# One state in sixteen of a selective scan joins its neighbour's tile on VectorE before TensorE sums them

## The reference

```python
dA = jnp.exp(dt[..., None] * A)                       # 512 positions x 512 features x 16 states
dBu = dt[..., None] * Bmat[:, :, None, :] * h[..., None]

def step(state, inp):
    Ai, dBui, Ci = inp
    state = Ai * state + dBui
    y = jnp.einsum('bhd,bd->bh', state, Ci)           # the sum over the 16 states, weighed by C
    return (state, y)
...
y = y + h * D
y = y * jax.nn.silu(gate)
return y @ W_out
```

## Time and profile before

| | us |
|---|---|
| median of three runs | 2609.22 |
| lowest and highest | 2605.43, 2614.64 |
| the profiled execution | 2597.4 |
| its span, first to last instruction | 2595.7 |
| PE busy | 2283.7 (88%) |
| DVE busy | 1753.1 (68%) |
| ACT busy | 1375.4 (53%) |
| POOL busy | 1336.9 (52%) |
| mean granted clock of TensorE | 0.94 |

### The profile page before, as it was taken

The page is one execution under the profiler, slowest core; times in us unless marked ns, Lnnn a source line. Parts: engine busy times, 40 slices in busy tenths (PEclk is TensorE's granted clock), DMA queues, the critical chain, the costliest instruction groups (busy, mean ns, idle before and its releaser), DMA issues.

```text
span 2595.7 us, 27201 instructions
## 1 busy us (share of the span) xinstructions
PE 2283.7 (88%) x8580; PEld 1482.4 (57%) x8580; DVE 1753.1 (68%) x2782; ACT 1375.4 (53%) x1816; POOL 1336.9 (52%) x1152
## 2 busy tenths in 40 slices
PE   2799989999899986688998998998998998998978
PEld 0466667667676652244654654655655655655667
DVE  3454455563645659798689689689689689688730
ACT  0234525435344363466766766766766766765622
POOL 1241432532514225566666666666666666657733
PEclk6889999999999997899999999998999999999989
DMA  7035555456345473555545545555555544546623
GB/s 247 14 94 164 171 188 169 157 163 188 128 138 158 161 212 110 131 142 145 164 131 157 163 129 151 164 136 141 162 143 145 163 141 138 167 130 170 191 67 97
DMA packets 253774, 384.79 MB, mean 148 GB/s; under 512 B 19168, under 2 KB 159984, under 8 KB 253632
## 3 DMA queue, kind: packets, MB, share of 16 engines
q1 hardware_dynamic: 223408, 281.33, 38.2%
q0 software_dynamic: 30224, 101.73, 12.6%
HBM read 345.93 MB, written 47.55 MB: 152 GB/s over the span
## 4 chain that ended last, share of the span: by engine, by line
PE 48%; DVE 17%; issue 12%; POOL 9%; ACT 7%; DMA 2%; DVEq 0%; POOLq 0%; SPq 0%; ACTq 0%
PE bank L233 20%; PE bank L239 8%; PE bank L240 7%; PE bank L1535 7%; DVE bank L1457 4%; DVE w_st L1465 4%; POOL d_in L1447 3%; POOL xs_rows L813 2%; POOL f1L L1613 1%; DVE cv L1275 1%; DMA bc<-bc_rows 1%; PE bank L718 1%; PE bank L720 1%; PE bank L719 1%; DVE mid L1637 1%
## 5 line engine op out<-in xcount | busy, mean ns | idle before, releaser
L1447 POOL TENSOR_TENSOR d_in<-u,bc 128x512 f32<-128x512 f32 x512 | 656.4, 1292 | 376.2 <-DMA bc<-bc_rows 299.5
L1457 DVE TENSOR_TENSOR_SCAN bank<-bank,d_in 128x512 f32<-128x512 f32 x512 | 625.2, 1222 | 101.4 <-ACT bank L1513 60.2
L1535 PE MATMUL bank<-w_st,ident 128*128 128x512 f32 x1024 | 540.6, 642 | 87.4 <-DVE w_st L1465 87.1
L1513 ACT ACTIVATE bank<-dt,a_neg 128x512 f32<-128x512 f32 x512 | 348.5, 689 | 453.9 <-DVE w_st L1465 452.1
L1465 DVE TENSOR_TENSOR w_st<-bank,bc 128x512 f32<-128x512 f32 x512 | 344.7, 673 | 118.8 <-PE bank L1535 118.5
L239 PE MATMUL bank<-f1H,w_ring 128*128 128x512 f32 x768 | 360.4, 469 | 50.7 <-ACT raw L1344 21.7
L1535 PEld LDWEIGHTS bank<-w_st,ident 128*128 128x128 f32 x1024 | 194.6, 199 | 306.6 <-DVE w_st L1465 179.2
L240 PE MATMUL bank<-f1L,w_ring 128*128 128x512 f32 x768 | 311.7, 406 | 0.0
L239 PE MATMUL bank<-f0H,w_ring 128*128 128x512 f32 x512 | 228.5, 446 | 3.6 <-POOL f0L L1613 3.6
L1613 POOL TENSOR_TENSOR f0L<-mid,f0H 128x512 fp32r<-128x512 f32 x128 | 170.4, 1332 | 112.8 <-DVE f0H L1641 78.1
L239 PEld LDWEIGHTS bank<-f1H,w_ring 128*128 128x128 f32 x768 | 151.5, 197 | 128.3 <-issue 77.7
(11 more groups left out here) (210 smaller groups left out, 3978.5 us busy)
## 6 DMA issues: line engine op xcount, KB each, us to landing
bc<-bc_rows SPq DMA_DIRECT2D x256, 512.0 KB, 5.1
w_ring<-w_units POOLq DMA_DIRECT2D x160, 512.0 KB, 4.3
w_exp<-L_ffn_ew SPq DMA_DIRECT2D x240, 256.0 KB, 4.5
eo_rows<-eo SPq DMA_DIRECT2D x56, 256.0 KB, 4.3
xs<-xs_rows SPq DMA_DIRECT2D x24, 512.0 KB, 4.0
w_units<-h_T SPq DMA_DIRECT2D x16, 512.0 KB, 6.5
xA<-L_attn_x SPq DMA_DIRECT2D x8, 512.0 KB, 6.1
x_mid<-xA SPq DMA_DIRECT2D x8, 512.0 KB, 2.8
```

Source lines behind the costliest of these rows:

```text
L1447: pool.tensor_tensor(d_in[:, nth(b, s) % IN, :], u[:, c, :], rows_tile(b, use)[:, 0, :], ALU.mult).then_inc(in_made.sem, 1)
L1457: dve.tensor_tensor_scan(bank[:, :], bank[:, :], d_in[:, nth(b, s) % IN, :], 0.0, ALU.mult, ALU.add).then_inc(scanned.sem, 1)
L1513: act.activation(state_bank(b, s)[:, :], dt[:, c, :], ACT.Exp, scale=a_neg[:, c, n:n + 1]).then_inc(dA_made.sem, 1)
L1535: pe.matmul(y_bank(c)[:, :], ident[:, :], w_st[:, nth(b, s) % WG, :], start=False, stop=(n == NST - 1)).then_inc(summed.sem, 1)
```

## The change

For state 7 (`FOLDED`) PE's sum is left out. DVE adds its weighed tile to the weighed tile of state 8 of the same features, two steps later, and PE sums the joined tile. That is 4 tiles in each batch and 32 in all: steps 14, 15, 46 and 47 have no sum, and steps 16, 17, 48 and 49 have an addition on DVE behind their weighing. The addition waits for the weighing just ahead of it on its own engine, and PE's sum of those four steps waits for the addition (`joined`) instead of the weighing. `sums` and `joins` count how often each semaphore has been raised up to a step.

Besides, some pairs of semaphores become one (`c_step`, `a_step`, `q_step`, `k_step`, and `sim_neg` goes into `sim_max`). Their waits ask for the same instructions as before.

```diff
+            FOLDED = (7,)
+            dA_made, in_made, scanned, weighed = (signal(n, STEPS) for n in ("dA_made", "in_made", "scanned", "weighed"))
+            summed, joined = signal("summed", STEPS - len(FOLDED) * KI), signal("joined", len(FOLDED) * KI)
...
+            def folded(s):
+                return step(s)[0] in FOLDED
+
+            def sums(s):
+
+                return sum(not folded(i) for i in range(s + 1))
+
+            def joins(s):
+                return sum(folded(i) for i in range(s + 1 - HC))
...
                     if nth(b, s) >= WG:
                         before, old = step_back(b, s, WG)
-                        dve.wait_ge(*summed.at(before, old + 1))
+                        if folded(old):
+                            dve.wait_ge(*joined.at(before, joins(old + HC)))
+                        else:
+                            dve.wait_ge(*summed.at(before, sums(old)))
                     dve.tensor_tensor(w_st[:, nth(b, s) % WG, :], state_bank(b, s)[:, :], rows_tile(b, step(s)[2])[:, 1, :], ALU.mult
                                       ).then_inc(weighed.sem, 1)
+                    if s >= HC and folded(s - HC):
+                        now, last = w_st[:, nth(b, s) % WG, :], w_st[:, nth(b, s - HC) % WG, :]
+                        dve.wait_ge(*weighed.at(b, s + 1))
+                        dve.tensor_tensor(now, now, last, ALU.add).then_inc(joined.sem, 1)
...
-                    pe.wait_ge(*weighed.at(b, s + 1))
+                    if folded(s):
+                        continue
+                    if s >= HC and folded(s - HC):
+                        pe.wait_ge(*joined.at(b, joins(s)))
+                    else:
+                        pe.wait_ge(*weighed.at(b, s + 1))
                     pe.matmul(y_bank(c)[:, :], ident[:, :], w_st[:, nth(b, s) % WG, :], start=False, stop=(n == NST - 1)
                               ).then_inc(summed.sem, 1)
```

More of the change, by code:

```diff
@@ L262, in adaln_kernel @@
         c_in, wmod_in = signal("c_in", 32), [signal(f"wmod{l}_in", 16) for l in range(2)]
-        c_act_made, cT_made = signal("c_act_made"), signal("cT_made")
+        c_step = signal("c_step", 2)
         mod_made = signal("mod_made")
@@ L344, in adaln_kernel @@
             qk_done, qk_biased, qk_act = signal("qk_done", TT), signal("qk_biased", TT), signal("qk_act", TT)
-            q_scaled, q_made = signal("q_scaled", TT), signal("q_made", TT)
-            k_scaled, k_made = signal("k_scaled", TT), signal("k_made", TT)
+            q_step, k_step = signal("q_step", 2 * TT), signal("k_step", 2 * TT)
             hid_done, hid_act = signal("hid_done", 2 * KH), signal("hid_act", 2 * KH)
-            sim_done, sim_max, sim_neg, sim_exp = (signal(n, KH) for n in ("sim_done", "sim_max", "sim_neg", "sim_exp"))
+            sim_done, sim_max, sim_exp = signal("sim_done", KH), signal("sim_max", 2 * KH), signal("sim_exp", KH)
             asum_step, gated = signal("asum_step", 2), signal("gated", KH)
@@ L461, in setup_tensor @@
                 pe.wait_ge(consts_made.sem, 2)
-                pe.wait_ge(*c_act_made.all(0))
+                pe.wait_ge(*c_step.at(0, 1))
                 for l in range(2):
@@ L467, in setup_tensor @@
                 i.then_inc(modT_turned.sem, 1)
-                pe.wait_ge(*cT_made.all(0))
+                pe.wait_ge(*c_step.all(0))
                 for l in range(2):
@@ L517, in decay_rates_scalar @@
                 act.wait_ge(a_log_in.sem, 16)
-                act.activation(a_neg[:, :, :], a_neg[:, :, :], ACT.Exp).then_inc(a_exped.sem, 1)
+                act.activation(a_neg[:, :, :], a_neg[:, :, :], ACT.Exp).then_inc(a_step.sem, 1)
             def decay_rates_vector():
                 yield x1_at(1) + PLAN_A["rates"] + 2
-                dve.wait_ge(*a_exped.all(0))
-                dve.tensor_scalar(a_neg[:, :, :], a_neg[:, :, :], -1.0, None, ALU.mult).then_inc(a_made.sem, 1)
+                dve.wait_ge(*a_step.at(0, 1))
+                dve.tensor_scalar(a_neg[:, :, :], a_neg[:, :, :], -1.0, None, ALU.mult).then_inc(a_step.sem, 1)
                 dve.wait_ge(ssm_weights_in.sem, 5 * 16)
@@ L644, in att_pool @@
                     yield x1 + 5 + t
[L645 removed]
+                    pool.wait_ge(*q_step.at(b, t + 1))
                     if b == 0 and t == 0:
                         pool.wait_ge(qk_weights_in.sem, 6 * 16)
[L648 removed]
+                    pool.tensor_tensor(k_tok[:, t, :], k_tok[:, t, :], os_rows[:, 1, 0, :], ALU.mult).then_inc(k_step.sem, 1)
                 for t in range(TT):
                     yield x1 + 7 + t
[L651 to L652 removed]
+                    pool.wait_ge(*k_step.at(b, t + 1))
+                    pool.tensor_tensor(k_tok[:, t, :], k_tok[:, t, :], os_rows[:, 1, 1, :], ALU.add).then_inc(k_step.sem, 1)
             def att_scalar(b):
@@ L724, in att_tensor @@
                     if d == 0:
-                        pe.wait_ge(*q_made.all(b))
-                        pe.wait_ge(*k_made.all(b))
+                        pe.wait_ge(*q_step.all(b))
+                        pe.wait_ge(*k_step.all(b))
                     products(tile(14 + d)[:, :], lambda t: q_tok[:, t, d * P:(d + 1) * P], lambda t: k_tok[:, t, :], TT
@@ L1156, in adaln_kernel @@
             bc_stored, bc_in = buffer_signal("bc_stored", 2), buffer_signal("bc_in", BC)
-            dA_made, in_made, scanned, weighed, summed = (signal(n, STEPS) for n in
-                                                          ("dA_made", "in_made", "scanned", "weighed", "summed"))
+            FOLDED = (7,)
+            dA_made, in_made, scanned, weighed = (signal(n, STEPS) for n in ("dA_made", "in_made", "scanned", "weighed"))
+            summed, joined = signal("summed", STEPS - len(FOLDED) * KI), signal("joined", len(FOLDED) * KI)
             y_gated = signal("y_gated", KI)
@@ L1463, in weigh @@
                         before, old = step_back(b, s, WG)
-                        dve.wait_ge(*summed.at(before, old + 1))
+                        if folded(old):
+                            dve.wait_ge(*joined.at(before, joins(old + HC)))
+                        else:
+                            dve.wait_ge(*summed.at(before, sums(old)))
                     dve.tensor_tensor(w_st[:, nth(b, s) % WG, :], state_bank(b, s)[:, :], rows_tile(b, step(s)[2])[:, 1, :], ALU.mult
                                       ).then_inc(weighed.sem, 1)
+                    if s >= HC and folded(s - HC):
+                        now, last = w_st[:, nth(b, s) % WG, :], w_st[:, nth(b, s - HC) % WG, :]
+                        dve.wait_ge(*weighed.at(b, s + 1))
+                        dve.tensor_tensor(now, now, last, ALU.add).then_inc(joined.sem, 1)
                 def gate_output(c):
-                    dve.wait_ge(*summed.at(b, (c // HC + 1) * HALF))
+                    dve.wait_ge(*summed.at(b, sums((c // HC + 1) * HALF - 1)))
                     dve.wait_ge(*gate_made.at(b, c + 1))
@@ L1507, in core_scalar @@
                         if b == 0 and s == 0:
-                            act.wait_ge(*a_made.all(0))
+                            act.wait_ge(*a_step.all(0))
                             act.wait_ge(*s2_out.all(B - 1))
```

22 lines of the change are left out of this document (9 added, 13 removed).

## The result

The changed kernel takes 2633.7 us (median of 4 runs, 2630.91 to 2639.68); before, 2609.28 (4 runs, 2605.43 to 2614.64). The ratio is 1.0105, 95% interval 1.0081 to 1.013: slower, by 24.4 us in the medians and by 27 us by the ratio. The forecast was 2624, range 2602 to 2643. The profiled execution took 2639.68 us, its span is 2637.6 us, and its mean granted clock 0.928 (before 0.940).

What follows compares the result with a forecast made beforehand. DVE was taken to set the first halves, PE's chain the second, with DVE hardly ahead. 6 x (1.1 + 1.0) + 1.5 + 1.1 - 0.2 = 15.0 us more, so a median of 2624, range 2602 to 2643.

Steps and rivals of the forecast that it cites:

- The direction and the mechanism: Whole kernel: slower by 6 to 20 us, as PE waits for the addition in second halves; chance 0.45.
- PE's work is what counts: Rival, whole kernel: less PE work gains time, about 2597 us, at the very best 2582; chance 0.2.
- The wait at step 48: Second halves: PE, done with step 45's sum at 1664.13, waits for the addition until 1666.1, or 1666.85 if POOL holds it.
- The term of 1.0 us for the wait itself: Second halves of six batches: 0.25 to 1.0 us lost each despite two removed sums of 1.71 us; 1.0 taken.
- POOL's hold: Addition of step 48: with two SBUF inputs it ends 0.54 us behind POOL's instruction, taking 1.45 us.
- The mean of the 32 additions: Sign for the forecast: additions average 0.8 to 1.2 us, the longer ones where POOL runs.
- The clock: Behind the wait at step 48: half clock for 3.4 us costs 1.7; only in the range, 0 to 10 us.
- The row of 2.05 us idle followed by half clock: Profile before, in front of 1653.19: PE idled 2.05 us, then 3.40 us ran at a granted clock of 0.51.
- the ends: First batch 1.5 us more; last batch 1.1 more in its first half and 0.2 gained in its second.
- First halves: Six batches: additions of steps 16 and 17 delay DVE's work, 1.1 us each, bounds 0.7 to 1.4.
- PE's busy time: Sign for the forecast, whole kernel: PE's busy time falls by about 25 us, and the time doesn't.
- The merged semaphores: Whole kernel: they ask for the same instructions, so they cost and give nothing.

Runs made afterwards that it cites:

- e4_remove_only: Kernel before with merged semaphores, the 32 sums of state 7 left out and nothing added in their place (output lacks that state): 1.0009 of before.
- e6_psum_add: Changed kernel, but the weighings to be joined write back into their PSUM bank, so the addition has one input in SBUF: 1.0068 of before, 2621.12 us.
- e5_add_only: Changed kernel with its 32 additions and all sums of state 7 kept too (output counts it twice): 1.0093 of before, 2624.01 us against 2602.09.
- e1_sem_only: Changed kernel with no state folded, only the merged semaphores left: 1.0024 of before, 2604.75 us.
- e2_first_half: Changed kernel with state 7 folded only in the first half of each batch: 1.0025 of before.
- e3_second_half: Changed kernel with state 7 folded only in the second half of each batch: 1.0085 of before.
- e7_fold_5_10: Changed kernel with states 5 and 10 folded instead of state 7, in the second halves alone, again 32 sums: 1.0108 of before.

## Why the prediction was right, and where it was off

**The direction and the mechanism** were right. PE's work was not what counts at either place. e4_remove_only shows it: 1.0009 with 27 us of it gone. What counts in the second halves is the wait for the addition, as forecast, and the clock behind it. The rival "PE's work is what counts" falls with it.

**The wait at step 48.** Forecast: the addition takes 1.45 us, PE waits until 1666.85, from 1664.13, so 2.7 us. Measured: 1.40 and 2.75 us. The term of 1.0 us for the wait itself (2.75 less the 1.71 us of the two sums) was right in four batches of six.

**POOL's hold.** Right in kind, shown by e6_psum_add, and too small in two batches. The forecast took one POOL instruction as the longest hold. Four in a row made 4.99 us, and PE waited 5.87 us instead of 2.75, 3.1 more. These halves are only 1.7 us longer than the others, 101.5 instead of 99.8, because the clock behind their wait for `f1L` stayed up, which gives back 1.6. So the long hold costs about 6 us outside the sum in the two, and some 3 of them came back by luck. The mean of the 32 additions, 0.8 to 1.2 us by the forecast, is 1.26 us with these two and 1.01 without.

**The clock** is the term that was mis-sized: 0 in the sum, 0 to 10 us in the range. It fell behind each of the six waits of 2.74 to 5.88 us. A second half of 99.8 us is 2.9 us longer than before: 1.0 for the wait and the rest, 1.9, nearly all for the stretch at half clock (e5_add_only, without it: 1.6 less). Six times this is about 10 us, the upper end of what I had left to the range. The row of 2.05 us idle followed by half clock was the nearest one, and with a wait forecast at up to 2.7 us half clock was the likelier level. It was not certain: this wait for `f1L` was followed by full clock in three of six halves of e1_sem_only.

**The sum.** 15.0 forecast, made of 6 for the second halves, 6.6 for first halves, and 2.4 for the ends. Measured: 20.7 us in the six second halves, which are 6 for the wait, 10 for the clock, 3 for the long hold after what came back, and a remainder of some 2; 6.5 to 11.1 us in all eight first halves, where 9.2 were forecast (with the 1.5 of the first batch). The timed runs say 24.4 in the medians.

**The range.** Its upper ends do not follow from its own terms. The bounds that it names add up to 2615 to 2628, not 2631, and with 10 us for the clock to 2638, not 2643. The measured 2633.7 lies between the two: outside without the clock, inside with it.

**First halves.** The cost is of the size forecast by the lengths of the halves. The timed runs don't confirm it: e2_first_half has 1.0025, e1_sem_only without a fold 1.0024. The additions of the first batch cost little (99.9 and 79.8 us after, 100.2 and 79.2 before). In the last second half 0.2 us was to be gained; PE waited 1.58 us for the addition there, and the half is 0.9 to 1.2 us longer.

**PE's busy time** was to fall by 25 us and fell by 4.4. The count of instructions fell as it should. Busy time is measured in us, and more of the matmuls now run at half clock: in the stretch above PE had 9 records where 17 fitted before. This sign was a bad one: it mixes work with clock.

**The merged semaphores**: no cost shown. Their two measurements, 1.0024 and 1.0009, leave room for up to 0.3 or 0.4%, as much as the first halves.

**Open.** Why the hold lasts for one POOL instruction in four batches and for four in two. The three long holds (one is in e3_second_half) stand in just those halves in which the clock behind the wait for `f1L` stayed up, and POOL's order differs there (`f0L` ahead of `d_in`). But `f0L` ahead doesn't make a hold long by itself: in e7_fold_5_10 it was ahead six times with holds of 1.77 to 1.79 us, and beside two `d_in` the addition took 3.02 to 3.04 us four times. No run changed that order alone. What decides whether the clock falls behind an idle stretch of some 2 us is open too.

## What to carry to other kernels

Before taking work off a busy engine, find what it does next: if the next instruction waits for another engine, the time freed turns into idle time (here 1.71 us into 1.53), and the idle time can bring the matmuls behind it down to half clock. A tile that a second engine is to join belongs where that engine is ahead, and its addition should read at least one input from PSUM when GpSimd works beside it, and only there: the bank stays taken for longer, and what reuses it has to wait. A fold that fits once (state 10, 0.9975) needn't fit twice (1.0064).

## What the runs showed of the hardware

- A VectorE addition of two 128x512 float32 tiles in SBUF takes 0.69 us alone, ended 0.55 us behind one POOL instruction in a first case (1.40 us), and behind the last of four in a row in a second (4.99 us; three times in two kernels). Beside two it took 3.03 us. With one input in PSUM it took 0.69 us 32 times out of 32, in 19 of which a POOL instruction was running when it started. I hadn't expected VectorE to be kept out across several instructions of POOL.
- The clock behind an idle stretch of PE, in front of a hidden layer's matmuls or of the sum ahead of one, isn't told by the length of the stretch alone. Stretches of 1.03 us (e5_add_only), 1.22 us (before) and 1.53 us (e4_remove_only) were followed by a granted clock of 1.00. Stretches of 2.05 us (before), 2.19 (e6_psum_add) and 2.75 (after) were followed by 0.51 to 0.53. But 2.00 us (e1_sem_only), 2.04 (after, sixth batch) and 2.14 (e6_psum_add) were followed by 1.00. One stretch at half clock made a half 1.6 us longer (96.9 us against 95.3 in e1_sem_only). For e4_remove_only the row is this one:

```profile
1667.00:1670.40 3.40, 3.40 (x16) 2.65 (x15) 3.40 (x5) 1.82 (x3) 3.40 (x3) 1.00 0.40 92
```
